# Filler matmuls in TensorE's two waits before the gathering of the first expert mixture

## The reference

```python
xn = xf / rms * norm_weight                       # xf: 1024 tokens x 128
logits = xn @ router_weight.T + router_bias       # 1024 x 16
probs = softmax(logits, axis=-1)
_, idx = top_k(logits.T, 64)                      # every expert draws 64 of 1024 tokens
xe = xn[idx]                                      # their rows, gathered
h = gelu(einsum('ecd,efd->ecf', xe, fc1_weight) + fc1_bias[:, None, :])
y = einsum('ecf,edf->ecd', h, fc2_weight) + fc2_bias[:, None, :]
gates = take_along_axis(probs.T, idx, axis=1)
output = zeros.at[idx].add(y * gates)             # then divided by the summed gates
```

## Time and profile before

| | us |
|---|---|
| timed runs: median, lowest, highest | 555.09, 555.05, 558.54 |
| profiled execution | 552.32 |
| its span, first to last instruction | 550.3 |
| PE busy | 478.3 |
| DVE busy | 372.1 |
| ACT busy | 223.6 |
| POOL busy | 193.3 |

### The profile page before, as it was taken

One profiled execution on the slowest core, in us unless ns is written; L12 is line 12 of the kernel. 1 busy time (PEld: TensorE's weight loads), 2 busy tenths in 40 slices (PEclk: granted clock), 3 DMA queues, 4 the chain that ended last, 5 costly groups with the idle time before them and its releaser, 6 DMA issues. The chain is left out here.

```text
span 550.3 us, 10856 instructions
## 1 busy us (share of the span) xinstructions
PE 478.3 (87%) x3971; PEld 243.8 (44%) x3971; DVE 372.1 (68%) x918; ACT 223.6 (41%) x453; POOL 193.3 (35%) x334
## 2 busy tenths in 40 slices
PE   2899898998988998988648998878999889999995
PEld 1435344443433433333213988335423334466664
DVE  7545775877766868666887475665679784366565
ACT  1411345355564664767100220522416666624221
POOL 7552737665446437048210002840544000000001
PEclk9999999999998999999878999899999999999999
DMA  7221202134544012000704022000331000350700
GB/s 249 67 59 50 60 1 69 51 88 140 180 136 101 12 51 60 4 2 2 305 1 146 11 88 88 1 0 1 85 89 35 27 3 3 95 137 2 229 21 20
DMA packets 27108, 38.05 MB, mean 69 GB/s; under 512 B 3808, under 2 KB 19744, under 8 KB 26672
## 3 DMA queue, kind: packets, MB, share of 16 engines
q1 hardware_dynamic: 27056, 37.36, 22.3%
HBM read 23.91 MB, written 0.59 MB: 45 GB/s over the span
## 5 line engine op out<-in xcount | busy, mean ns | idle before, releaser
L1098 DVE TENSOR_REDUCE nmax<-bank 128x2 f32<-128x512 f32 (+2 forms) x240 | 144.6, 624 | 76.9 <-PE bank L867 34.1
L979 ACT ACTIVATE arena<-bank 128x512 f32<-128x512 f32 (+2 forms) x256 | 131.0, 527 | 122.1 <-PE bank L871 84.3
L867 PE MATMUL bank<-arena 62*128 62x256 bf16 (+2 forms) x512 | 86.4, 258 | 10.9 <-DVE nmax L1098 5.6
L509 PE MATMUL bank<-causal_qk,identb 128*128 128x512 bf16 x270 | 79.9, 400 | 11.0 <-DVE y L1043 5.4
L871 PE MATMUL bank<-arena 64*128 64x256 bf16 (+2 forms) x512 | 85.9, 256 | 2.2 <-ACT arena L979 1.5
L912 PE MATMUL bank<-arena 128*32 128x256 f32 (+4 forms) x1088 | 72.9, 346 | 8.6 <-ACT arena L979 3.1
L867 PEld LDWEIGHTS bank<-arena 62*128 62x128 bf16 x512 | 29.8, 94 | 77.5 <-issue 48.5
L734 POOL TENSOR_SCALAR_AFFINE_SELECT arena<-arena 128x256 f32<-128x256 f32 x64 | 25.7, 409 | 49.3 <-ACT arena L979 48.5
L509 PEld LDWEIGHTS bank<-causal_qk,identb 128*128 128x128 bf16 x270 | 22.5, 101 | 43.6 <-issue 10.8
L871 PEld LDWEIGHTS bank<-arena 64*128 64x128 bf16 x512 | 30.2, 94 | 16.7 <-issue 7.0
L912 PEld LDWEIGHTS bank<-arena 128*32 128x32 f32 x1088 | 21.4, 109 | 34.6 <-issue 18.9
(11 more groups left out here) (318 smaller groups left out, 817.4 us busy)
## 6 DMA issues: line engine op xcount, KB each, us to landing
arena<-arena SPq DMA_DIRECT2D x96, 128.0 KB, 2.4
fcw<-in_fc1T SPq DMA_DIRECT2D x16, 256.0 KB, 3.7
arena<-in_fc2T SPq DMA_DIRECT2D x1, 4096.0 KB, 12.4
arena<-comb_rows SPq DMA_DIRECT2D x16, 256.0 KB, 4.3
fcw<-in_last SPq DMA_DIRECT2D x1, 2304.0 KB, 8.0
arena<-pos_rows SPq DMA_DIRECT2D x16, 128.0 KB, 2.9
arena<-comb_rows SPq DMA_DIRECT2D x16, 128.0 KB, 4.2
w<-in_w SPq DMA_DIRECT2D x1, 1216.0 KB, 6.3
```

Of the source, the lines that this page charges most:

```text
L509: nc.tensor.matmul(bank[:, :], m.identb[:, :], m.causal_qk[:, 0:4, :], start=True, stop=True)
L867: mins = t.matmul(mout[:, i, :], stack_rows(m, nm, h0 + i, 0, MAX_ROWS)[:, qt * P:(qt + 1) * P], stack_rows(m, nm, h0 + i, 1, MAX_ROWS)[:, ...
L979: s.activation(m.prob[h % 8][:, 0:w], score_bank(n, h)[:, 0:w], ACT.Exp).then_inc(exps, 1)
L1098: v.tensor_reduce(m.nmax[n % 2][:, qt, h0:h0 + nh], MX[c % NMX][:, 0:nh * (k1 - k0)].rearrange("p (h k) -> p h k", h=nh), AX.X, ALU.max, n ...
```

## The change

Two calls of `keep_warm` are added on PE: 8 fillers between the counting matmuls and the wait for `pos_ready`, and 5 between the transposes and the waits of the gathering. Lines behind them move by one and by two: L1354 becomes L1355, L1362 becomes L1364, L1407 becomes L1409.

```diff
-F_ROUTE = 18
+F_ROUTE, F_PLACED, F_GATHER = 18, 8, 5
@@ tensor_on
         t.matmul(B[2][:, 0:2], before_it[:, :], ranks[:, :, SEQ - 1], start=True, stop=False, skip_group_check=True)
         t.matmul(B[2][:, 1:2], of_expert[:, :], ranks[:, 0, SEQ - 1:SEQ], start=False, stop=True, skip_group_check=True).then_inc(count_mm, 1)
+        keep_warm(nc, m, B[7], F_PLACED)
         pe.wait_ge(pos_ready, 1)
         for q in range(QT):
             t.transpose(B[5][:, q * P // 2:(q + 1) * P // 2].bitcast(BF16), posb[:, q * P:(q + 1) * P],
                         m.identb[:, :]).then_inc(posT_mm, 1)
 
+        keep_warm(nc, m, B[7], F_GATHER)
         pe.wait_ge(xnl_ready, 2)
         for i in range(TILES):
             pe.wait_ge(oh_ready, i + 1)
```

## The result

The changed kernel's median is 553.73 us over 20 runs, against 555.25 us over 20 runs of the kernel before; by the runs compared it takes 0.9937 of the time, 95% interval 0.9912 to 0.9961. Four of the changed kernel's twenty runs, 559.55 to 564.81 us, are left out of that ratio as disturbed, and none of the kernel before, though five of its runs lie between 558.01 and 560.81. The medians of all runs stand at 0.9973, a difference of 1.52 us. Either way the difference lies within the 1% that was called no change.

The account below looks back on a forecast made before the run. DVE was taken to set the end before the gathering and PE from there on, the gathering starting at half clock. Fillers priced at nothing, a held clock at 1.33 us: 555.09 us less 1.33 gives 553.7, range 550.4 to 557.0.

Parts of the forecast that it names:

- What bounds the stretch: DVE sets the end before the gathering, PE from 289.99 us on; a shorter gathering's 1.33 us go through to the end.
- The eight fillers, free with 0.5 us of cover: After the count, eight fillers at 0.216 us fit the 2.35 us wait; transposes still start at 287.99.
- The five, free with 0.6 us: After the transposes, five fillers take 1.08 us and end at 289.35, before the comparison releases the gathering at 289.99.
- No slowing of DVE: PE traffic does not slow DVE: MATCH_REPLACE8 took 464 ns beside earlier fillers, 462 ns without PE work.
- The clock holds: With some 3.3 us of PE work in 5.4 us before the gathering, the granted clock stays at 1.00.
- two windows that pointed both ways: PE busy 1.52 of 3.40 us with full-width fillers, level stayed; busy 2.22 with small attention matmuls, level fell.
- 1.33 us: Gain from a held clock: the gathering's 48 matmuls take 10.53 us and end at 300.52 instead of 301.85.
- the upper bound, half of 3.90 = 1.95 us: Largest gathering gain in other executions, from the rise 3.90 us after the F_ROUTE fillers began.
- The slower rival: The eight after the count run at the lower level, transposes come 1.05 us late: 556.5 us, chance 0.07.
- The larger-gain rival: Gathering's slow part longer in timed runs, or the later recurrence also profits: 2.2 us, 552.9 us, chance 0.12.
- The median: Whole kernel: 1.33 us taken off the 555.09 us median of three timed runs, forecast 553.7 us.

Follow-up runs that it names:

- The second timing: The changed kernel, unchanged, timed and traced again: 554.40 us over 12 runs, ratio 0.9981 against the kernel before.
- the run made to show it: Against the changed kernel, the 18 fillers before the count left out, the 8 and the 5 kept: 553.78 us over 10 runs, ratio 0.9979.

## Why the prediction was right

- **What bounds the stretch.** Right. A shorter gathering brought all that follows forward by as much: in every trace the stretch from the gathering's end to the first transposes of the recurrence is 40.24 us, to 0.01.
- **The eight fillers, free with 0.5 us of cover.** Right: 0.60 us of wait were left, and doubling them cost 0.9 us.
- **The five, free with 0.6 us.** Right: 0.64 us left.
- **No slowing of DVE.** Right: 2.80 us from count to first comparison in both kernels.
- **The clock holds.** Right in four traces of four. The step was argued from two windows that pointed both ways, and took the one with full-width work. The fillers with 32 rows bear out that choice: with PE busy for 2.83 of the 3.35 us behind the count they did not hold it, where full ones held it with 2.75 of the same 3.35.
- **1.33 us.** Right for the trace on which it was made (1.34), too small for others. Three traces without the change's fillers have 16.42, 18.00 and 17.40 us from the count to the gathering's end, four with them 15.07 to 15.08: 1.3, 2.9 and 2.3 us, mean 2.2. The ratio of the first timing points the same way: its interval of 0.9912 to 0.9961 is 2.2 to 4.9 us, above 1.33. The second timing, 0.9981 (0.9949 to 1.0013), leaves 1.33 possible. The step that was mis-sized is the upper bound, half of 3.90 = 1.95 us: it took the longest slow stretch of the rows around the gathering, but in the second trace of the kernel before 5.94 us of the gathering were slow, which at 0.425 us each are 14 matmuls. The count of 14 that the Trainium skill gives as the highest of its three (TensorE: Matmul & The Clock Gate, Part 1) agrees with that trace.
- **The slower rival.** Its price per filler was right (0.95 us measured, 1.05 forecast), its total was not: 556.5 us assumed that the gathering gets nothing back and that the five add 0.3 to 0.4. In the run made to show it both were wrong, and it came to 553.78 us. In that one trace the clock rose 0.66 us ahead of the gathering. What a later rise would cost was not seen, but here the change did not end behind the kernel before even with slow fillers.
- **The larger-gain rival.** Its second half looked at the recurrence and priced the fall there at the one DVE wait of the earlier trace rows, 0.26 us. The fall that matters comes behind it, on the hidden products, and was not in the trace at hand: 84.9 instead of 81.3 us for the stretch to L789, 3.6 us, more than the change itself. It is no gain of this change, though: the changed kernel's second trace has it as well.
- **The median.** 553.7 forecast, 553.73 measured; with a term of 1.3 where the traces say 2.2, a starting median of three runs (555.09) where twenty have 555.25, and a scatter of over 3 us between runs, that close a hit is luck.

## What to carry to other kernels

A wait of PE ahead of a dense stretch can cost that stretch its clock even where the wait itself is hidden, as the two waits of 2.35 and 1.72 us did here. Fill it with matmuls of full width, no more of them than the wait holds, and check in the trace that the next real instruction still starts when its operand is ready. Where waits follow each other closely, fill them all: here one group of fillers did not hold the clock in one trace each, and both did in four. Where single runs scatter by more than the edit is worth, compare the length of the touched stretch between two fixed instructions over several traces, and look in the other traces for falls that the first did not have: here the larger prize lay there.

## What the runs showed of the hardware

- The clock can fall while PE is working densely, behind the idle time and not in it: 0.78 us after the gathering had begun in the run with the 8 alone.
- The same code lost 1.34 us in one execution and 2.92 in another: the slow stretch around the gathering was 3.41 us long in the first and 6.82 in the second (287.02 to 293.84), and began 0.67 and 0.88 us ahead of it.
- PE's busy time alone does not tell where the clock goes: in the 3.35 us from the count on, fillers of 32 rows kept PE busy for 2.83 us and the clock fell, and fillers of 128 rows for 2.75 us and it held. This is one pair of traces. Fillers of either width follow each other at the same pace, eight in 1.89 us.
